# Expert loops over 43 tiles in place of 44 in a fused transformer kernel

## The reference

```python
xf = x.reshape(-1, Dm)                      # 2048 tokens of 128
ys = _geglu(xf @ Ws1 + bs1) @ Ws2 + bs2     # shared expert, all tokens
logits = (xf @ Wr + br) / TAU               # 12 experts
top_val, top_idx = jax.lax.top_k(logits, 2) # each token goes to two
top_w = jax.nn.softmax(top_val, axis=-1)
...
h = jnp.einsum('nd,edh->enh', xf, We1) + be1[:, None, :]   # 128 -> 768
act = _geglu(h)                                            # 768 -> 384
yE = jnp.einsum('enh,ehd->end', act, We2) + be2[:, None, :] # 384 -> 128
yr = jnp.einsum('end,ne->nd', yE, w)
```

## Time and profile before

| | |
|---|---|
| median of 3 runs | 1385.63 us (1384.06 to 1387.5) |
| profiled execution | 1376.06 us, of it 1374.3 us from the first instruction to the last |
| phase 0, first gather to last scatter's issue | 962.8 to 1103.6 us |
| phase 1, the same | 1208.8 to 1351.5 us |
| indirect DMAs on POOL | 176: 44 gathers and 44 scatters in each phase |
| `x_up` matmuls (L1845) | 1056 in both phases, 141.3 us |

### The profile page before, as it was taken

The page is one execution under the profiler, slowest core; times in us unless marked ns, Lnnn a source line. Parts: engine busy times, 40 slices in busy tenths (PEclk is TensorE's granted clock), DMA queues, the critical chain, the costliest instruction groups (busy, mean ns, idle before and its releaser), DMA issues.

```text
span 1374.3 us, 36568 instructions
## 1 busy us (share of the span) xinstructions
PE 1173.4 (85%) x12741; PEld 878.2 (64%) x12742; DVE 929.1 (68%) x2485; ACT 847.7 (62%) x2486; POOL 798.1 (58%) x712
## 2 busy tenths in 40 slices
PE   5899898998879999799989899898787858768784
PEld 2667675766745555467668566685687836457773
DVE  6988669986846777688866988688332367633233
ACT  3999768998435555489985899843243524313343
POOL 6788348884654352388744878443666532266653
PEclk9999999999989999999999999998899989879998
DMA  7011100111000000001110001132365520135564
GB/s 220 18 25 25 28 15 13 28 26 28 15 2 3 4 3 3 2 10 30 26 28 17 9 21 25 35 78 77 109 182 160 173 69 0 49 108 168 169 189 118
DMA packets 70226, 79.26 MB, mean 58 GB/s; under 512 B 25191, under 2 KB 50598, under 8 KB 69926
## 3 DMA queue, kind: packets, MB, share of 16 engines
q1 hardware_dynamic: 64421, 65.49, 17.2%
q0 software_dynamic: 5632, 11.55, 3.0%
HBM read 55.52 MB, written 8.91 MB: 47 GB/s over the span
## 4 chain that ended last, share of the span: by engine, by line
PE 33%; DVE 7%; ACT 6%; issue 4%; DMA 4%; POOL 2%; POOLq 1%; SPq 1%; another core or an unknown queue 1%; ACTq 0%; DVEq 0%
PE bank L1845 10%; PE bank L1859 4%; ACT pB L791 3%; PE bank L912 3%; DMA arena<-arena 2%; PE bank L633 1%; PE bank L924 1%; PE bank L596 1%; PE bank L541 1%; PE bank L555 1%; DVE mx L717 1%; PE bank L547 1%; POOL arena L2202 1%; PE bank L1786 1%; PE bank L1833 1%
## 5 line engine op out<-in xcount | busy, mean ns | idle before, releaser
L2105 DVE SCALAR_TENSOR_TENSOR act_b<-bank,vec,gl 128x128 f32<-128x128 f32 x264 | 76.8, 345 | 185.9 <-PE bank L1845 94.9
L860 POOL TENSOR_TENSOR rn<-ss,mhalf 128x16 f32<-128x16 f32 x64 | 187.8, 2934 | 6.7
L1929 ACT ACTIVATE gl<-bank,vec 128x128 f32<-128x128 f32 x264 | 77.9, 366 | 127.3 <-PE bank L1845 101.6
L1845 PE MATMUL bank<-arena 128*128 128x128 f32 x1056 | 141.3, 286 | 3.3 <-DVE act_b L2105 2.2
L1845 PEld LDWEIGHTS bank<-arena 128*128 128x128 f32 x1056 | 131.6, 200 | 10.1 <-issue 5.8
L2182 POOL DMA_INDIRECT arena<-u_rows,inv_u x88 | 87.0, 988 | 69.7 <-remote 33.3
L791 ACT ACTIVATE pA<-bank,nb,rn 128x128 f32<-128x128 f32 x256 | 113.7, 485 | 3.1 <-DVE nb L722 3.1
L791 ACT ACTIVATE pB<-bank,nb,rn 128x128 f32<-128x128 f32 x256 | 113.4, 477 | 1.7 <-DVE nb L722 1.7
L2188 POOL DMA_INDIRECT y_rows<-stg,inv_u x88 | 87.6, 996 | 42.9 <-ACT stg L1936 22.7
L846 POOL TENSOR_TENSOR arena<-arena 128x512 f32<-128x512 f32 x64 | 81.7, 1276 | 46.2 <-DVE nb L722 35.4
L853 POOL TENSOR_TENSOR arena<-arena 128x512 f32<-128x512 f32 x64 | 81.4, 1272 | 43.0 <-DVE arena L685 16.4
(11 more groups left out here) (335 smaller groups left out, 3140.8 us busy)
## 6 DMA issues: line engine op xcount, KB each, us to landing
arena<-in_L_ffn_We SPq DMA_DIRECT2D x88, 384.0 KB
arena<-arena SPq DMA_DIRECT2D x64, 128.0 KB, 2.3
arena<-in_L_ffn_We SPq DMA_DIRECT2D x3, 768.0 KB, 7.2
arena<-U SPq DMA_DIRECT2D x32, 64.0 KB
u_rows<-U SPq DMA_DIRECT2D x2, 1024.0 KB, 6.0
U<-y_rows SPq DMA_DIRECT2D x8, 256.0 KB, 4.4
uT<-y_rows SPq DMA_DIRECT2D x8, 256.0 KB, 4.6
arena<-U SPq DMA_DIRECT2D x32, 63.5 KB
```

The costliest lines, as they stand in the source:

```text
L860: pool.tensor_tensor(rn[:, q % 4, :, :], ss[:, 1, :].rearrange("p (a h) -> p a h", a=2), mhalf[:, :].rearrange("p (a h) -> p a h", a=2), A ...
L1845: m = pe.matmul(bank[q % 2][:, j * P:(j + 1) * P], we1[q][:, half * HR + j * P:half * HR + (j + 1) * P], xT[:, q, :], start=True, stop=True)
```

## The change

A new constant NU is the most tiles that 4096 rows of twelve experts can fill: (4096 - 128) // 128 + 12 = 43. All five engines' tile loops, the semaphore base of phase 1 and the counts of loads go from NXT to NU. The tables keep NXT = 44 columns, so the routing is unchanged. Since 43 tiles don't divide by four, the count per semaphore becomes a function `quarter(q)`: 11, 11, 11 and 10. On PE, tile 43's place in the last group keeps only `x_down` of tile 41.

```diff
 NXT = (2 * NT * P) // P + E
-NXG = NXT // 4
+NU = (2 * NT * P - P) // P + E
+
+def quarter(q):
+    return (NU - q + 3) // 4
...
-            kc, base = k0 * NCH, k0 * NXT
+            kc, base = k0 * NCH, k0 * NU
...
                     n = 8 * i + 4 * o + q
-                    x_up(i, o, q)
+                    if not (isinstance(i, int) and n >= NU):
+                        x_up(i, o, q)
...
-                    if not (isinstance(i, int) and n + 2 >= NXT):
+                    if not (isinstance(i, int) and n + 2 >= NU):
...
-            with pe.Fori(OCT, NXT // 8) as i:
+            with pe.Fori(OCT, NU // 8) as i:
...
-            group(NXT // 8, 0)
-            x_down(NXT // 8, 0, 2)
-            x_down(NXT // 8, 0, 3)
+            group(NU // 8, 0)
+            x_down(NU // 8, 0, 2)
...
-            for n in range(NXT + LAG):
-                if n < NXT:
+            for n in range(NU + LAG):
+                if n < NU:
                     gather(n)
...
-            for n in range(NXT):
+            for n in range(NU):
                 if n >= WB:
                     sp.wait_ge(s.x_up, 2 * (base + n - WB + 1))
...
-            for sem in (s.st_y0, s.st_y1, s.st_y2, s.st_y3):
-                sp.wait_ge(sem, 16 * NXG * (k0 + 1))
+            for q, sem in enumerate((s.st_y0, s.st_y1, s.st_y2, s.st_y3)):
+                sp.wait_ge(sem, 16 * quarter(q) * (k0 + 1))
```

More of the change, by code:

```diff
@@ L1773, in x_loads @@
         def x_loads(k0, buf):
-            return k0 * (NXT // XG + (buf < NXT % XG))
+            return k0 * (NU // XG + (buf < NU % XG))
         def expert(eng, n):
@@ L1836, in x_up @@
                 n = 8 * i + 4 * o + q
-                pe.wait_ge((s.ld_e0, s.ld_e1, s.ld_e2, s.ld_e3)[q], 16 * (NXG * k0 + 2 * i + o + 1))
+                pe.wait_ge((s.ld_e0, s.ld_e1, s.ld_e2, s.ld_e3)[q], 16 * (quarter(q) * k0 + 2 * i + o + 1))
                 pe.wait_ge(s.x_T, base + n + 1)
@@ L1933, in y_out @@
                 act.wait_ge(s.x_dn, base + n + 1)
-                if n + k0 * NXT > 3:
-                    act.wait_ge((s.st_y0, s.st_y1, s.st_y2, s.st_y3)[n % 4], 16 * (NXG * k0 + n // 4))
+                if n + k0 * NU > 3:
+                    act.wait_ge((s.st_y0, s.st_y1, s.st_y2, s.st_y3)[n % 4], 16 * (quarter(n % 4) * k0 + n // 4))
                 act.activation(yb[:, n % 4, :], XY[n % 2][:, 0:D], ACT.Copy).then_inc(s.x_y, 1)
@@ L1947, in mx_act @@
             x_out(1)
-            for n in range(NXT + 2):
-                if n < NXT:
+            for n in range(NU + 2):
+                if n < NU:
                     gelu(n, expert(act, n))
@@ L1952, in mx_act @@
                     y_out(n - 2)
-                if n + 2 < NXT:
+                if n + 2 < NU:
                     x_out(n + 2)
@@ L2216, in mx_sync @@
         def mx_sync(sp, k0):
-            base = k0 * NXT
+            base = k0 * NU
             if not k0:
```

## The result

The kernel with 43 tiles took 1373.95 us, the median of eight runs (1369.39 to 1379.3), against 1384.6 us for eight runs of the kernel before (1381.8 to 1388.61). The ratio is 0.993 with an interval of 0.9912 to 0.9947, by that ratio a saving of 9.7 us (7.3 to 12.2). The profiled execution went from 1376.06 to 1371.62 us.

A forecast was written before the change was run, and what follows sets the result against it. POOL's gather issues were taken to pace the middle of the expert phases. Two phases' 6.58 us plus 0.33 us from drains gave 6.9 us, taking the median from 1385.63 to 1378.7 us, range 1375.8 to 1382.6 (own range 1376.8 to 1381.0).

The forecast's parts named there:

- What bounds the kernel: Expert phases: POOL's four back-to-back issues and a gap pace the middle, 6.17 us a pair, until the last gather.
- Steps 1 and 2: End of each phase: one fast tile, 2.01 us, plus POOL's last row one issue shorter, 1.28 us; together 3.29 us.
- The fast end: Last tiles of a phase, behind the last gather: PE always busy, tiles 2.12 us apart, the last two 2.01 us.
- the gap: Late `x_up` behind POOL's last unbroken row: 3.62 us after its forerunner in phase 1, expected to fall to 2.34 us.
- Step 3: Behind each phase's last `x_up`: the work there moves up with PE's last tile, nothing hides the saving; price 0.
- Step 4: POOL's two long drains: 0.083 us per indirect DMA, two fewer save 0.17 us each, 0.33 us in all.
- Step 5: Semaphore counts, weight buffers and `x_loads`: the same instructions with other numbers; price 0.
- A: End of phases: only a fast tile goes, the late `x_up` stays as late; 4.35 us saved, 1381.3 us; chance 0.16.
- C: PE's loop in phase 1 lies elsewhere, jumps back wait for instruction fetches; 3.2 us remain, 1382.4 us; chance 0.10.
- D: Phase 1 meets the clock differently and half-clock falls hit more pairs; 5.5 us slower with seven, 1391.1 us; chance 0.05.
- B: Both phases: late `x_up` not late at all, and one clock fall missed in phase 1; 9.4 us, 1376.2 us; chance 0.07.
- steps 2 and 4: Bounds: shorter last POOL row wins 0 to 1.50 us in phase 1, 0 to 1.72 in phase 0; drains 0 to 0.33.

The follow-up runs named there:

- the loop written out: Kernel before, 44 tiles, with the last of three rounds of PE's loop (tiles 32 to 39) written out: 1383.29 us, ratio 1.0005.
- 42 tiles, three kernels: 42 tiles in both phases, run, repeated, and with PE's last loop round written out, against the kernel before: 1365.67, 1364.88 and 1366.89 us.
- 43, drained early: Changed kernel plus one more POOL drain behind the last scatter of each phase: 1369.97 us, ratio 0.991 to the kernel before.
- 44, drained early: Kernel before plus one more POOL drain behind the last scatter of each phase: 1375.41 us, ratio 0.9947.
- the one with small weights: Kernel before with the first weights of every tile from the fifth on cut from 384 to 4 KB: 1383.6 us, ratio 1.0002.

## Why the prediction was right in kind and too small

- **What bounds the kernel: right.** Taking the gathers off POOL brings the middle to the pace of the end, and cutting the weights' traffic doesn't. One sum in it is off without effect: four issues end to end are 4.83 us by the earlier trace rows (1323.33 to 1328.16), not 5.1, and it is these that make 6.16 us with the idle 1.33.
- **Steps 1 and 2, 3.29 us per phase: right in sum.** The fast end's 2.01 us is there again. In the first pair of traces the gap shrank by 1.25 us in phase 0, as forecast, and by 0.54 in phase 1. Over 24 phases the 44th tile costs 20.95 - 17.86 = 3.1 us. The one gap was a weak row to rest on, since it wanders from 2.1 to 4.0 us with the same kernel, and that the sum came out from it as well as it did is in part luck.
- **Step 3, nothing hides it: right.** From phase 0's last `x_up` to phase 1's first gather it takes 110.2 us in both early traces of the change and 111.1 in the third, against 111.5, 111.1, 111.8 and 110.8 before. By the means that is 0.8 us less, so nothing was held back.
- **Step 4, 0.33 us: right.** The drain between the phases follows the count of indirect DMAs in every trace, below. The program's last drain falls with the count too, but strays by 0.13 us without it.
- **Step 5, 0 us.** No trace shows anything to the contrary.
- **Rivals.** A (the gap stays) is out: the end saves 3.1 and not 2.0 us. C is out: the six branches of the changed kernel took 76 to 242 ns as before, and the loop written out gives 1.0005. The rule on fetches behind it, in the Trainium skill, page "Runtime: NRT & Kernel Launch", section "Instruction fetch mechanics", had no price in any run here. D is out: the mean granted clock was 0.955 before and 0.953 after, and phase 1 got shorter by 1.5 us (136.4 to 134.9). B's time, 1376.2, lies nearest to what was measured, but its mechanism isn't what did it: the gap is 2.75 and 3.08 us in the first trace, not 2.12. Of ten phases with 43 tiles one had no late `x_up` at all (16.84 us from tile 34 on); the mean has 17.86.
- **The step that failed** is the one behind the sum: "The median of the runs, 1385.63, lies 9.6 us above it, and I take the saving over unchanged: 1378.7 us", with the range that was put about it. 1378.7 is 4.1 us above the change's mean of 1374.6. Of that, 1.9 is the base: the median of three runs stood at 1385.63, where 71 runs have a mean of 1383.7 with a standard deviation of 3.3. Three runs don't tell the level closer than about 4 us, and the range allowed 0.5 for it. The other 2.2 is the saving: 9.1 in timed runs against 6.9. The range had a slip of its own besides: the bounds of steps 2 and 4 widened by 0.5 give 1377.6 to 1382.1, not 1376.8 to 1381.0.

Those 2.2 us were not located as work of the kernel. The table has every difference by means, against all runs of the kernel before and against those taken beside the kernel in question, with the mean granted clock of the timed runs. Over 62 runs of the kernel before, that clock is 0.9474 on average.

| kernel | runs | less than all | less than those beside it | granted clock |
|---|---|---|---|---|
| 43 tiles | 19 | 9.1 | 9.9 | 0.949 |
| 43 in phase 0 alone | 12 | 4.0 | 4.6 | 0.948 |
| 43 in phase 1 alone | 12 | 3.1 | 3.7 | 0.948 |
| 42 tiles, three kernels | 13 | 18.2 | 17.7 | 0.950 |
| 40 tiles | 6 | 22.9 | 23.5 | 0.945 |
| 43, drained early | 5 | 13.6 | 13.1 | 0.951 |
| 44, drained early | 6 | 8.4 | 7.9 | 0.953 |

The two phases cut alone give 7.1 or 8.3 together, the drained pair of kernels 5.3, the profiled executions 7.0, the stages of the traces 6.5 and perhaps 0.5 more between them. The direct comparison gives 9.1 with 1.7 either way. A value near 8 fits all of them within their errors. Half of the 2.2 us goes with the clock: the runs of the change had it 0.0017 higher, and at about 0.7 us for each 0.001 that is 1.2 us, so at equal clock the change saves about 8. In the same way the 5.3 of the drained pair becomes about 7, since the kernel with 44 tiles ran at 0.9533 and the one with 43 at 0.9508. Whether the clock is the cause or only a sign of it isn't shown.

The runs with 42 tiles lie further off. Their timed mean is 1365.5, where the stages of the traces, 2 x (20.95 - 14.98) + 0.65 = 12.6 us less than before, give 1371.1. The clock takes about 1.5 us of the difference. But among profiled executions nothing is missing: those with 42 tiles took 1365.96, 1364.87 and 1366.89 us, 12.0 less than the 1377.9 of before. The offset of some 6 us is one between the timed runs (1383.7) and the profiled executions (1377.9) of the kernel before, which the 42-tile kernels don't have (1365.5 and 1365.9). Nor have two other kernels with 44 tiles, the one with small weights (1383.4 timed, 1382.31 profiled) and the one with the loop written out (1383.7 and 1386.27), so it may be an accident of few executions. Neither the loop (1.0005) nor the repeat explains it, and at 40 tiles it doesn't show in the saving (22.2 by the stages, 22.9 timed). Whether it sits in the 959 to 967 us ahead of the tiles, where most of the difference between executions of one kernel lies, stays open.

## What to carry over

Where one loop has a slow middle and a fast end, a removed iteration is worth the fast price plus what the border between them moves, and that is read as a mean over several traces, not from one gap. A forecast in absolute time also needs the level: a base of three runs carries its own error into the range, however well the mechanism is known. The base and the changed kernel are best read at like granted clocks and in like executions, profiled with profiled. And a queue that must be drained is better drained where its engine is idle anyway.

## What the runs showed of the hardware

- **GpSimd's drain is owed per indirect DMA.** Behind 88, 86, 84, 80 and 44 of them it took 8.32, 8.16, 8.00, 7.67 and 4.73 us: 1.14 us and 0.082 us for each, for DMAs of 128 rows, gathers or scatters. That is the drain between the phases. The program's last drain is about 0.35 us longer and less regular: 8.55 or 8.68 us behind 88. The row for 44, from the kernel whose gathers SP loads:

```profile
L315 POOLq DRAIN  x4: 816/1642/4732, 375.9 to 1135.1; - x4
```

- **It can be paid early.** A drain of 9.1 to 9.5 us during other engines' work leaves 1.1 us for the next.
- **With indirect gathers issued on POOL between the scatters the whole tile loop is slower,** 3.1 against 2.12 us a tile, though POOL's products are not what PE waits for by name. Replacing the 88 gathers by plain loads on SP saved 88 us, the shorter drains included. Which part of a gather does it is open.
- **Run time goes with the granted clock.** Over 62 runs of the kernel before, the time falls by about 0.7 us for each 0.001 of mean granted clock (correlation -0.7), around a mean of 0.947. That the clock sets the time isn't shown by it.
